# The token chain ahead of cross-attention in two groups beside self-attention, with transposes, V and K of the context in the last self-attention steps, and the second layer's last q one unit earlier

## The chip, the cores and the metric

The kernel runs on one core of one Trainium2 chip. The metric is the device time of one execution in microseconds, in the median of several runs. Engines are named as in the profile: PE is TensorE (PEld its weight loads), DVE is VectorE, ACT is ScalarE, POOL is GpSimd, SP is the engine that issues most of the DMAs.

## What is computed

There are 8 units (batch entries) with 56 latent rows of 128 channels each, and a context of 1500 rows per unit. Everything is float32, with 16 heads of 8 channels:

```python
x = x + mha(ln(x), ln(x))                    # self-attention, 56 rows with 56 rows of the same unit
x = x + mha(ln_q(x), ln_kv(ctx))             # cross-attention, 56 rows with 1500 rows
h = ln(x); gates = softmax(top2(h @ rw.T + rb))
x = x + sum_e gates[e] * (gelu(h @ fc1[e].T) @ fc2[e].T + b2[e])     # 8 experts
x = x + attn(ln(x), ctx; bit_quant(Wq, Wk, Wv, Wo))                  # second cross-attention
```

## The kernel before

The 448 latent rows lie in four token tiles of 112 rows, so that a tile holds two units: tile 0 has units 0 and 1. Each engine has a program written out by hand, and semaphores tie the programs together; an engine takes its instructions strictly in their order, and a wait holds up all that is queued behind it.

**Self-attention** runs in `SA_STEPS` = 12 steps. In step i the scores of batch i are made, batch i-1 is transposed, batch i-2 is multiplied with the values, batch i-3 is transposed back and normalised, and batch i-4 comes out as columns of `attnT`. The table `SA_PIECES` puts work on the context between these: "t" is `transpose_ctx` of a third of a unit, "k" is `project_k` of a third. A piece's first instruction on PE waits until the last user of the bank `MI` has been evacuated (`prev`). DVE and POOL do the statistics of the context (`ctx_stats`, `ctx_aggregate`, `ctx_rstd`, `ctx_normalise`) between steps. K is split into three bf16 parts by ACT, POOL (`k_rest`), DVE (`k_second_part`) and POOL (`k_third_part`, which counts `k3_done`). When all three thirds of a unit are split, SP copies them by `restack` in two halves of six DMAs into `kst`.

**The first chain** follows for all four token tiles at once: `project_out(0)`, `add_projection(0)`, `token_stats(1)`, `token_rstd(1)`, `token_normalise(1)`, `transpose_tokens(1)`, `token_gain(1)`, `project_q(0)`, `split_q(0)` into three bf16 parts, `load_qall(0)` (six DMAs on SP) and `place_q` into `qst` for unit 0. PE also makes K of unit 1 here (`project_k_apart`).

**The start of the pass** makes `START_TILES` = 18 of unit 0's 24 maximum tiles (`max_tile` on PE, `reduce_tile` on DVE, four banks). V of unit 0 and the transposes of unit 2 stand between them. After tile 11 `max_parts` gives the maxima of the first half, `transpose_max` turns them after tile 15, and a DMA (`shift`) puts them beside q. The scores wait for it.

**A window** is the cross-attention of one unit in 12 steps: scores, exponentials, values, with the maximum tiles of the next unit (`STEP_TILES`; in the first window `FIRST_TILES`, which also has what is left of unit 0's), K of the unit after next in steps 0 to 2, V of the next in steps 4 to 6, and in the first layer transposes of a later unit in steps 9 to 11. On SP a window issues `place` and `restack` of the next unit's second half, a context load, and `place` and `restack` of the first half of the unit after it. `max_tile` waits at tile 0 and at tile 12 for the `kst` half that it reads. Eight windows make the first layer's pass, the experts follow, and eight windows the second's. There the last half of q (`split_q(2)`, `load_qall(2)`) is made in windows 1 and 2; unit 4 is the first to need it.

## Time and profile before

| | us |
|---|---|
| median of 3 runs | 582.97 (581.22 to 584.65) |
| the profiled execution | 581.15 |
| its span in the trace | 579.4 |
| PE busy | 528.1 (91%) |
| PE weight loads | 391.9 (68%) |
| DVE busy | 391.7 (68%) |
| ACT busy | 334.0 (58%) |
| POOL busy | 220.5 (38%) |

The share of the chain that ended last is 70% PE and 15% DVE. Matrix work on PE overlaps, so that its busy share is not its share of peak. The granted clock of PE is given as a part of full speed (1.0 is 2.4 GHz, 0.5 is 1.2 GHz); it is 0.946 over the whole span, and below full in the first quarter and in the slice around 456 us. In timelines, several like instructions in a row are merged into one row with their count, and the brackets at a row's end give how long the engine had stood and what ended it.

### The profile page before, as it was taken

The page shows a single profiled execution, that of the slowest core. Times are in us where ns is not written, and L with a number is a line of the kernel's source. Part 1 is how long each engine was busy: PE and PEld are TensorE (multiplying, and loading weights), DVE is VectorE, ACT ScalarE, POOL GpSimd, SP SyncE. Part 2 cuts the span into 40 slices and gives each one's busy share as a digit, 9 for nine tenths or more (in the row PEclk, how much of TensorE's full clock was granted, in tenths as well). Part 3 has the DMA queues.
Part 4 walks back from the last instruction along what each step waited for, and adds up shares of the span by engine and source line. Part 5 has one row for each costly group of instructions (what it writes and reads, how often), then busy time and mean ns, then how long its engine had stood idle before and what let it go on. Part 6 is the DMA issues. An engine that isn't in the chain of part 4 may idle for free.

```text
span 579.4 us, 16262 instructions
## 1 busy us (share of the span) xinstructions
PE 528.1 (91%) x6648; PEld 391.9 (68%) x6648; DVE 391.7 (68%) x976; ACT 334.0 (58%) x527; POOL 220.5 (38%) x217
## 2 busy tenths in 40 slices
PE   4699748789999999999989999999999899999996
PEld 2588525466767676776767998867677576767674
DVE  6565477767878888787742434888878477786730
ACT  1156322547686777766676444376666467675573
POOL 3549944473957677532251200031403032240000
PEclk9679877889999999999999999999999799999997
DMA  5110361734444554647546601005372826534300
GB/s 157 48 54 3 107 148 44 174 92 101 122 119 104 137 139 90 155 95 190 146 107 185 175 2 28 5 0 141 86 187 57 218 57 166 135 88 101 76 4 9
DMA packets 37870, 58.69 MB, mean 101 GB/s; under 512 B 17957, under 2 KB 21405, under 8 KB 37797
## 3 DMA queue, kind: packets, MB, share of 16 engines
q1 hardware_dynamic: 37476, 57.60, 39.5%
q8 instruction: 53, 0.87, 0.6%
q14 instruction: 21, 0.16, 0.1%
q10 hardware_dynamic: 320, 0.06, 0.1%
HBM read 17.81 MB, written 0.23 MB: 31 GB/s over the span
## 4 chain that ended last, share of the span: by engine, by line
PE 70%; DVE 15%; POOL 4%; DMA 3%; issue 3%; ACT 2%; SPq 2%; ACTq 0%; DVEq 0%; POOLq 0%
PE SM L1371 13%; PE PO L1386 13%; PE ST L1343 9%; DVE mxp L883 8%; PE MI L1292 8%; PE MI L1282 7%; PE ST L1564 4%; PE ST L1554 4%; PE MI L1271 2%; POOL cxs L518 2%; PE SM L1477 2%; DVE ksplit L878 1%; ACT pts L671 1%; DMA xT<-in_ctxT 1%; PE MI L1318 1%
## 5 line engine op out<-in xcount | busy, mean ns | idle before, releaser
L883 DVE TENSOR_REDUCE mxp<-SM 112x1 f32<-112x500 f32 x374 | 244.5, 674 | 77.5 <-PE SM L1371 76.3
L671 ACT ACTIVATE pts<-ST 128x896 f32<-128x896 f32 x192 | 171.3, 912 | 29.4 <-PE ST L1343 29.0
L1371 PE MATMUL SM<-kst,qst 96*112 96x500 bf16 x374 | 146.9, 401 | 11.6 <-DVE mxp L883 6.7
L527 POOL TENSOR_TENSOR kr<-kf,ksplit 128x500 f32<-128x500 f32 x48 | 54.9, 1144 | 173.1 <-ACT ksplit L636 173.1
L1343 PEld LDWEIGHTS ST<-qst,kst 98*128 98x128 bf16 x1536 | 95.5, 100 | 36.3 <-issue 12.4
L1343 PE MATMUL ST<-qst,kst 98*128 98x112 bf16 x1536 | 108.3, 214 | 2.2 <-DMA qst<-mrow 2.2
L1386 PE MATMUL PO<-pts,vaug 125*32 125x112 f32 x3072 | 97.3, 266 | 2.0 <-ACT pts L671 1.6
L1386 PEld LDWEIGHTS PO<-pts,vaug 125*32 125x32 f32 x3072 | 71.4, 111 | 24.3 <-issue 14.7
L1371 PEld LDWEIGHTS SM<-kst,qst 96*112 96x112 bf16 x374 | 48.5, 131 | 45.4 <-DVE mxp L883 29.1
L518 POOL TENSOR_SCALAR cxs<-cxs,cmv,crstd 125x128 f32<-125x128 f32 x84 | 66.8, 810 | 0.0
L648 ACT ACTIVATE vaug<-MI 125x512 f32<-125x512 f32 x48 | 28.7, 597 | 60.8 <-PE MI L1292 60.8
L532 POOL TENSOR_TENSOR ksplit<-kr,ksplit 128x500 bf16<-128x500 f32 x48 | 54.4, 1135 | 16.7 <-DVE ksplit L878 16.7
L1292 PE MATMUL MI<-watt,xT 128*125 128x128 f32 x384 | 56.1, 291 | 0.3 <-ACT vaug L648 0.3
L1292 PEld LDWEIGHTS MI<-watt,xT 128*125 128x125 f32 x384 | 47.6, 193 | 8.9 <-issue 5.3
L1282 PE MATMUL MI<-xT,watt 128*128 128x500 f32 x92 | 49.6, 621 | 1.3 <-ACT ksplit L636 0.8
L635 ACT ACTIVATE kf<-MI,vec 128x500 f32<-128x500 f32 x46 | 31.1, 677 | 33.6 <-PE MI L1282 33.6
L769 ACT ACTIVATE moe<-ST,vec 128x224 f32<-128x224 f32 x64 | 28.4, 447 | 34.8 <-PE ST L1554 33.8
L878 DVE CAST ksplit<-kr 128x500 bf16<-128x500 f32 x48 | 34.8, 726 | 10.2 <-POOL kr L527 10.2
L636 ACT ACTIVATE ksplit<-MI,vec 128x500 bf16<-128x500 f32 x46 | 30.8, 670 | 0.0
L623 ACT ACTIVATE xT<-MI,vec 128x500 f32<-128x500 f32 x24 | 18.4, 767 | 16.3 <-PE MI L1271 15.8
L506 POOL TENSOR_TENSOR xrstd<-xvar,half_neg 112x2 f32<-112x2 f32 (+1 forms) x6 | 4.9, 809 | 59.9 <-DVE xvar L809 59.9
L511 POOL TENSOR_TENSOR crstd<-cvar,half_neg 125x12 f32<-125x12 f32 x8 | 18.3, 2287 | 22.5 <-DVE cvar L865 22.5
(156 smaller groups left out, 546.2 us busy)
## 6 DMA issues: line engine op xcount, KB each, us to landing
kst<-ksplit SPq DMA_DIRECT2D x192, 187.5 KB, 3.6
cxs<-in_ctx SPq DMA_DIRECT2D x8, 750.0 KB
xT<-in_ctxT SPq DMA_DIRECT2D x8, 750.0 KB, 6.5
qst<-qall SPq DMA_DIRECT2D x56, 21.0 KB, 1.9
watt<-in_watt SPq DMA_DIRECT2D x1, 768.0 KB, 6.0
cxs<-in_w1T SPq DMA_DIRECT2D x3, 256.0 KB, 5.7
cxs<-in_w2T SPq DMA_DIRECT2D x3, 256.0 KB, 6.7
pts<-in_w1T SPq DMA_DIRECT2D x3, 256.0 KB, 5.9
```

The source lines that it names most:

```text
L518: last = nc.gpsimd.tensor_scalar(cx[n.par][:, c], cx[n.par][:, c], cmv[n.par][:, c, 0:1], crstd[n.par][:, c:c + 1], ALU.subtract, ALU.mult)
L527: nc.gpsimd.tensor_tensor(kr[:, c], kf[:, c], ksplit[n.par][:, 0, c], ALU.subtract).then_inc(kr_done, 1)
L532: nc.gpsimd.tensor_tensor(ksplit[n.par][:, 2, c], kr[:, c], ksplit[n.par][:, 1, c], ALU.subtract).then_inc(k3_done, 1)
L635: nc.scalar.activation(kf[:, c], bank[:, 0:THIRD], ACT.Identity, bias=bias_k(n.s + 1)).then_inc(k_evac, 1)
L671: nc.scalar.activation(PT[:, k % PTB], ST[:, k % 2, :, 0:4 * PC], ACT.Exp, scale=SCALE).then_inc(exp_done, 1)
L878: nc.vector.tensor_copy(ksplit[n.par][:, 1, c], kr[:, c]).then_inc(k2_done, 1)
L883: nc.vector.tensor_reduce(mxp[:, j // 3, j % 3:j % 3 + 1], tile_bank(j, banks), AX.X, ALU.max).then_inc(sm_red, 1)
L1282: mm(bank[:, 0:THIRD], watt[:, n.s + 1, 1], xT[n.par][:, THIRD * i:THIRD * (i + 1)], start=True, stop=True).then_inc(kp_full, 1)
L1292: last = mm(MI[0:KC, D * c:D * (c + 1)], xT[n.par][:, at:at + KC], watt[:, n.s + 1, 2], start=True, stop=True)
L1343: last = mm(ST[:, k % 2, cc, PC * p:PC * (p + 1)], kst[n.par][:, 4 * half + p, at:at + 128], qst[n.par][:, 4 * half + p], start=True, stop ...
L1371: mm(tile_bank(j, banks), qst[n.par][0:SROWS, j // 3], kst[n.par][0:SROWS, j // 3, at:at + THIRD], start=True, stop=True).then_inc(sm_full, 1)
L1386: last = mm(PO[32 * p:32 * p + 32, PC * half:PC * (half + 1)], vaug[n.par][:, c, at:at + 32], PT[0:KC, k % PTB, cc, PC * p:PC * (p + 1)], ...
```

## The change

The first chain is cut into two groups (`PARTS`): token tile 0, and token tiles 1 to 3. The first group's steps stand in self-attention's steps 6 to 8: `project_out(0)` and the transposes of unit 1's first third in step 6, `transpose_tokens(1)` and `project_q(0)` in step 7, `split_q(0)` in step 8. `SA_PIECES` further takes the transposes of unit 1 in steps 6, 8 and 9, V of unit 0 in steps 8 to 10 and K of unit 1 in steps 10 and 11, one third each. On DVE `ctx_stats(u2)` moves from step 6 to 7 and its `ctx_aggregate` from step 7 to 8; POOL's `ctx_rstd(u2)` stays in its step 8, ahead of the last `k_third_part` of unit 0. The second group's steps stand between the maximum tiles of unit 0, of which there are now 21 ahead of the pass. SP issues `load_qall(0)` behind both halves of `restack(u0)`, then the context load of unit 3, and `load_qall(1)` behind `restack(u1, 0)`. The statistics of unit 3 move to tile 12 and to steps 3 and 4 of the first window. In the second layer the last q goes from steps (1,9) to (2,5) to steps (1,3) to (2,0), and `load_qall(3)` moves from the middle of SP's window 2 to the end of its window 1. The other lines renumber groups and semaphore counts, and are left out below.

```diff
 Q2_STEP, Q1_STEP = 1, 10
-START_TILES = 18
+START_TILES = 21
 def spread_tiles(own, per):
...
 OWN_MX_STEP, NEXT_MX_STEP = 1, 6
-FIRST_TILES = spread_tiles(TILES - START_TILES, (3, 3, 3, 3, 2, 2, 3, 3, 2, 2, 2, 2))
+FIRST_TILES = spread_tiles(TILES - START_TILES, (3, 3, 3, 3, 2, 2, 2, 2, 2, 2, 2, 1))
 FIRST_OWN_MX_STEP, FIRST_NEXT_MX_STEP = 3, 8
 OUT_AT, LN_AT, ROUTER_AT, GATES_AT, B2_AT = (5, 10), (6, 10), (6, 11), (7, 9), (7, 11)
-LN5_AT, Q2_AT = (1, 9), (1, 10)
-SPLIT2_AT = ((1, 11), (2, 4), (2, 5))
+LN5_AT, Q2_AT = (1, 3), (1, 9)
+START_OUT, START_ADD, START_NORM, START_LN, START_Q, START_SPLIT = 3, 3, 10, 12, 15, (16, 17, 18)
+SPLIT2_AT = ((1, 10), (1, 11), (2, 0))
 TERNARY_AT = ((4, 5), (4, 6), (4, 7), (4, 9), (4, 10), (4, 11), (5, 4), (5, 5), (5, 6), (5, 7), (5, 9))
...
 SA_PIECES = {1: (("t", 0, 0), ("t", 0, 1)), 2: (("t", 0, 2),), 3: (("k", 0, 0),), 4: (("k", 0, 1),),
-             5: (("k", 0, 2),), 7: (("t", 1, 0),), 8: (("t", 1, 1),), 9: (("t", 1, 2),)}
+             5: (("k", 0, 2),), 6: (("out", 0, 0), ("t", 1, 0)), 7: (("ln", 0, 0), ("q", 0, 0)),
+             8: (("t", 1, 1), ("v", 0, 0)), 9: (("t", 1, 2), ("v", 0, 1)), 10: (("v", 0, 2), ("k", 1, 0)),
+             11: (("k", 1, 1), ("k", 1, 2))}
 class Unit:
...
         window(Unit(s, None, u))
+PARTS = (range(0, 1), range(1, TT), range(0, HT), range(HT, TT), range(0, HT), range(HT, TT))
...
 def token_tiles(n):
-    return range(TT) if n < 2 else range(HT * (n % 2), HT * (n % 2 + 1))
+    return PARTS[n - 1] if n else range(TT)
...
+def token_slice(ts):
...
+    return slice(ts[0], ts[-1] + 1)
...
+def token_cols(ts):
...
+    return slice(TP * ts[0], TP * (ts[-1] + 1))
 def build_kernel(nc, x_in, ctx_in, ctxT_in, watt_in, vec_in, rows_in, rwT_in, w1T_in, w2T_in, b2_in,
...
             def load_qall(n):
-                cols = slice(0, N) if n == 0 else slice(HN * (n - 1), HN * n)
+                cols = token_cols(Q_TILES[n])
                 for part, ready in enumerate((q1_ready, q2_ready, q3_ready)):
...
             def place(n, half):
-                if n.s == 0 and n.c == 1:
-                    sp.wait_ge(qall_loaded, 16 * TERMS)
+                if n.s == 0 and n.c in (1, 2):
+                    sp.wait_ge(qall_loaded, 16 * TERMS * n.c)
                 if n.s == 1 and n.c in (1, B // 2):
-                    sp.wait_ge(qall_loaded, 16 * TERMS * (2 + n.c // (B // 2)))
+                    sp.wait_ge(qall_loaded, 16 * TERMS * (3 + n.c // (B // 2)))
                 if n.s or n.c >= 2:
...
                     restack(nxt, 1)
-                if n.s == 1 and n.c == 2:
-                    load_qall(2)
                 if n.s == 0 and (n + 4).exists():
...
                     load_xT(xT_unit)
+                if n.s == 1 and n.c == 1:
+                    load_qall(3)
                 if n.s == 0 and n.c in (3, 4):
...
             load_ctx(Unit(0, None, 2))
-            load_ctx(Unit(0, None, 3))
             restack(u0, 0)
...
             load_qall(0)
+            load_ctx(Unit(0, None, 3))
             place(u1, 0)
             restack(u1, 0)
+            load_qall(1)
             run_windows(0, window)
...
                     k_parts(k_unit, None)
+                if n.first():
+                    ctx_rstd(n + 3)
                 if n.s == 0 and (n + 3).exists():
...
                 if n.s == 0 and n.c == 5:
-                    token_rstd(2)
+                    token_rstd(3)
                 if n.s == 1 and n.c == 0:
-                    token_rstd(5)
+                    token_rstd(6)
             pool.wait_ge(padded, 1)
...
                     ctx_rstd(u1)
+                if i == 6:
+                    token_rstd(1)
                 if i == 8:
...
                     ctx_normalise(u1, (i - 4,))
-                if i in (9, 10):
-                    ctx_normalise(u0 + 2, (i - 9,))
+                if i == 9:
+                    ctx_normalise(u0 + 2, (0,))
                 for kind, unit, third in SA_PIECES.get(i - 1, ()):
-                    if kind == "k":
+                    if kind == "k" and unit == 0:
                         k_rest(u0, third)
                 for kind, unit, third in SA_PIECES.get(i - 3, ()):
-                    if kind == "k":
+                    if kind == "k" and unit == 0:
                         k_third_part(u0, third)
-            token_rstd(1)
+            k_parts(u1, None, lambda: ctx_normalise(u0 + 2, (1,)))
+            token_rstd(2)
             ctx_normalise(u0 + 2, (2,))
-            k_parts(u1, None)
-            ctx_rstd(u0 + 3)
             run_windows(0, window)
-            token_rstd(3)
+            token_rstd(4)
             gates_exp(1)
-            token_rstd(4)
+            token_rstd(5)
             run_windows(1, window)
...
                     evac_xT(n, (third,))
-                else:
+                if kind == "k":
                     evac_k(n, third)
+                if kind == "v":
+                    evac_v(n, third)
             for i in range(SA_STEPS):
...
                     evac_piece(*pieces[1])
-            for i in range(3):
-                evac_k(u1, i, K_BANKS[i])
             start_pass()
...
                 if half == 0:
-                    dve.wait_ge(qall_loaded, 16 * TERMS * (n.s + 1))
+                    dve.wait_ge(qall_loaded, 16 * TERMS * (2 * n.s + 1))
                     dve.wait_ge(ld_member, 32)
...
                 dve.wait_ge(op_full, n + 1)
-                t = slice(0, TT) if n == 0 else slice(HT * ((n - 1) % 2), HT * ((n - 1) % 2 + 1))
+                t = token_slice(PARTS[n])
                 width = D * (t.stop - t.start)
-                bank = MI if n in (1, 3) else PO
+                bank = PO if n % 2 else MI
                 nc.vector.tensor_tensor(xt[:, t], xt[:, t], bank[0:TP, 0:width].rearrange("p (t d) -> p t d", d=D),
...
                     if n.s == 1 and (n.c, k) == (0, 9):
-                        token_stats(5)
+                        token_stats(6)
                     if n.s == 1 and (n.c, k) == (0, 11):
-                        token_normalise(5)
+                        token_normalise(6)
                     if n.s == 1 and (n.c, k) == LN5_AT:
-                        token_gain(5)
+                        token_gain(6)
                     if n.s == 1 and (n.c, k) in SPLIT2_AT:
-                        split_q(2, (SPLIT2_AT.index((n.c, k)),))
+                        split_q(3, (SPLIT2_AT.index((n.c, k)),))
                     if n.s == 1 and (n.c, k) == OUT_AT:
-                        add_projection(3)
+                        add_projection(4)
+                    if n.first() and k == 3:
+                        ctx_stats(n + 3, range(6, NCH))
+                    if n.first() and k == 4:
+                        dve.wait_ge(cstat_ready, (n + 3).count(1, 1))
+                        ctx_aggregate(n + 3)
                     if ln_unit is not None:
...
                                             ).then_inc(sa_sub, 1)
+                if i == 6:
+                    add_projection(0)
+                    token_stats(1)
+                if i == 7:
+                    token_gain(1)
+                if i == 8:
+                    split_q(0)
                 if 0 <= i - 3 < B:
                     normalise(SM[:, 1], sa_pot, sa_rden, sa_norm, i - 2, i - 2, (i - 3) % 2)
+                if i == 6:
+                    token_normalise(1)
                 for kind, unit, third in SA_PIECES.get(i - 2, ()):
-                    if kind == "k":
+                    if kind == "k" and unit == 0:
                         k_second_part(u0, third)
...
                     ctx_aggregate(u1)
-                if i == 6:
+                if i == 7:
                     ctx_stats(u0 + 2, every)
-                if i == 7:
+                if i == 8:
                     dve.wait_ge(cstat_ready, (u0 + 2).count(1, 1))
                     ctx_aggregate(u0 + 2)
-            add_projection(0)
-            token_stats(1)
-            token_normalise(1)
-            ctx_stats(u0 + 3, range(5))
-            token_gain(1)
-            split_q(0)
-            ctx_stats(u0 + 3, range(5, NCH))
-            dve.wait_ge(cstat_ready, (u0 + 3).count(1, 1))
-            ctx_aggregate(u0 + 3)
...
             first = u0
             place_q(first, 0)
+            place_q(first, 1)
             for j in range(START_TILES):
                 reduce_tile(first, j, banks=4)
-                if j == 3:
-                    place_q(first, 1)
-                if j in (1, 4, 7):
-                    k_second_part(first + 1, j // 3)
+                if j == START_ADD:
+                    add_projection(1)
+                    token_stats(2)
+                if j == START_NORM:
+                    token_normalise(2)
+                if j == START_LN:
+                    token_gain(2)
+                if j in START_SPLIT:
+                    split_q(1, (START_SPLIT.index(j),))
+                if j in (0, 4, 7):
+                    k_second_part(first + 1, (0, 4, 7).index(j))
                 if j == TILES // 2 - 1:
                     max_parts(first, 0)
+                if j == TILES // 2:
+                    ctx_stats(u0 + 3, range(6))
             run_windows(0, window)
...
                 return v_evac, n.count(3, i + 1)
...
-            def project_k_apart(n, prev):
...
-                for i in range(3):
-                    last = project_k(n, i, prev, K_BANKS[i])
-                return last
             def transpose_max(n, half):
...
                     return transpose_ctx(n, third, prev)
-                return project_k(n, third, prev)
+                if kind == "k":
+                    return project_k(n, third, prev)
+                if kind == "out":
+                    pe.wait_ge(ld_rows, 48)
+                    return project_out(0, (sa_att, 2), prev)
+                if kind == "ln":
+                    return transpose_tokens(1, prev)
+                if kind == "q":
+                    return project_q(0, prev)
+                return project_v(n, third, prev)
             for i in range(SA_STEPS):
...
                     transpose_po(SM[:, 1]).then_inc(sa_pot, 1)
-            pe.wait_ge(ld_rows, 48)
-            project_out(0, (sa_att, B))
-            prev = project_k_apart(u1, prev)
-            transpose_tokens(1)
             pe.wait_ge(padded, 1)
             pe.wait_ge(ld_ones, 32)
-            project_q(0, 1)
...
             for j in range(START_TILES):
                 max_tile(u0, j, banks=4)
-                if j in (1, 4, 7):
-                    prev = project_v(u0, j // 3, prev)
-                if j in (10, 13, 16):
-                    prev = transpose_ctx(u0 + 2, (10, 13, 16).index(j), prev)
+                if j == START_OUT:
+                    project_out(1, (sa_att, B))
+                if j == START_LN - 1:
+                    prev = transpose_tokens(2, prev)
+                if j == START_Q - 1:
+                    prev = project_q(1, prev)
+                if j in (5, 8, 17):
+                    prev = transpose_ctx(u0 + 2, (5, 8, 17).index(j), prev)
                 if j == TILES // 2 + 3:
```

## Rows read from the trace of the kernel before

**Rows 1.** Windows: stretch, length, busy (count) per engine PE to POOL; clock, DMA, GB/s.

```profile
67.60:88.40 20.80, 11.76 (x29) 6.11 (x29) 10.97 (x47) 3.63 (x6) 11.36 (x14) 0.66 0.66 160
88.40:103.40 15.00, 12.10 (x55) 8.41 (x55) 12.67 (x26) 4.34 (x7) 6.74 (x5) 0.81 0.29 64
```

**Rows 2.** The chain that ended last, 67 to 104 us: start, length, step.

```profile
85.48 2.36 DMA qall<-qsplit
...
88.38 1.08 PE ST L1371 x2
...
99.67 0.22 PE ST L1308
...
100.19 3.18 DMA qst<-mrow
```

**Rows 3.** Timeline of POOL, 50 to 68 us: start, length, operation, idle before.

```profile
54.98 3.37 POOL L518 TENSOR_SCALAR cxs<-cxs,cmv,crstd 125x128 f32<-125x128 f32 x4
...
63.02 2.29 POOL L511 TENSOR_TENSOR crstd<-cvar,half_neg 125x12 f32<-125x12 f32 x1 [1.38 <-DVE cvar L865]
65.28 1.14 POOL L532 TENSOR_TENSOR ksplit<-kr,ksplit 128x500 bf16<-128x500 f32 x1
```

**Rows 4.** Timeline of SP's queue, 66 to 86 us.

```profile
66.44 9.86 SPq L412 DMA_DIRECT2D kst<-ksplit  x12
82.31 3.76 SPq L393 DMA_DIRECT2D qall<-qsplit  x6
```

**Rows 5.** Timeline of VectorE, 55 to 62 us.

```profile
55.36 2.41 DVE L855 BATCH_NORM_STATS2 cstat<-cxs 125x6 f32<-125x128 f32 x12
...
59.49 2.43 DVE L878 CAST ksplit<-kr 128x500 bf16<-128x500 f32 x1
```

**Rows 6.** Windows by stage: the six microseconds around and behind the first tile.

```profile
88.00:94.00 6.00, 5.62 (x22) 4.81 (x23) 4.29 (x11) 0.60 (x1) 2.22 (x2) 0.50 0.05 7
```

**Rows 7.** Timeline of TensorE in the first 90 us: pieces at half clock.

```profile
28.66 1.70 PE L1491 MATMUL ST<-ident,p_sa 112*56 112x112 f32 x8
...
67.74 0.74 PE L1234 MATMUL PO<-watt,attnT 128*112 128x128 f32 x2 [0.49 <-ACT attnT L740]
...
89.25 1.91 PE L1292 MATMUL MI<-watt,xT 128*125 128x128 f32 x8
```

**Rows 8.** Timelines of VectorE and POOL: reductions, and a subtraction beside POOL's.

```profile
97.66 1.25 DVE L883 TENSOR_REDUCE mxp<-SM 112x1 f32<-112x500 f32 x2
...
110.23 1.14 DVE L895 TENSOR_TENSOR mparts<-nmx,mparts 112x4 bf16<-112x4 f32 x1
...
110.22 1.13 POOL L527 TENSOR_TENSOR kr<-kf,ksplit 128x500 f32<-128x500 f32 x1 [1.59 <-ACT ksplit L636]
```

**Rows 9.** Timeline of TensorE, 415 to 457 us (second half).

```profile
415.67 1.14 PE L1292 MATMUL MI<-watt,xT 128*125 128x128 f32 x8
...
441.42 0.38 PE L1371 MATMUL SM<-kst,qst 96*112 96x500 bf16 x1
...
456.12 0.64 PE L1371 MATMUL SM<-kst,qst 96*112 96x500 bf16 x1 [2.13 <-issue]
```

**Rows 10.** Windows by stage: second half, windows of units 1 and 2.

```profile
407.21:431.99 24.78, 24.52 (x360) 17.49 (x359) 19.27 (x38) 16.59 (x26) 6.73 (x6) 1.00 0.52 127
431.99:461.50 29.51, 26.86 (x357) 18.13 (x356) 19.73 (x39) 17.01 (x26) 6.72 (x6) 0.90 0.60 145
```

**Rows 11.** Timeline of VectorE, 415 to 435 us.

```profile
415.12 1.34 DVE L878 CAST ksplit<-kr 128x500 bf16<-128x500 f32 x1 [0.17 <-POOL kr L527]
...
429.87 0.44 DVE L838 TENSOR_SCALAR qf<-MI,vec 128x224 f32<-128x224 f32 x1
...
431.67 2.67 DVE L883 TENSOR_REDUCE mxp<-SM 112x1 f32<-112x500 f32 x4
```

**Rows 12.** SP's queue at 434 us, and landing of `kst` copies, 420 to 460.

```profile
434.60 11.12 SPq L393 DMA_DIRECT2D qall<-qsplit  x6
...
DMA to landing us min/median/max: 2.8/3.8/5.0
```

96 lines of the change are left out of this document (46 added, 50 removed).

## The prediction

> **What bounds the kernel now.** I read from coarse to fine: the busy shares of the page, the busy time by stage, the chain of waits through the first 104 us, then the timelines of the engines on it. In the long middle TensorE is full, and a link shortened elsewhere is worth nothing there. The stages that the change touches are different: between 67.6 and 88.4 us TensorE is busy 11.76 of 20.80 us, and between 88.4 and 103.4 it is 12.10 of 15.00, at a granted clock of 0.81 [rows 1]. The reader is to see in the chain that this time is a row of small links: self-attention ends, the token chain follows, q is split, six `qall` copies are issued, the last lands 2.36 us after its issue at 85.48, and the first maximum tile is made at 88.38. At 99.67 the maxima of the first half are transposed, their shift takes 3.18 us by DMA from 100.19, and unit 0's scores follow at once, at 103.4 [rows 2]. So two things count at the start: when the first tile is made, and how long it is from there to the scores (15.0 us).
>
> **What gates the first tile after the change.** q of the first token tile is now early, but its `qall` copies stand on SP behind both halves of `restack(u0)`, which wait for `k3_done`, the last third part of unit 0's K. Before, that part ends at 65.28 + 1.14 = 66.42 [rows 3] and SP starts its twelve copies at 66.44 [rows 4]. On POOL it stands behind `ctx_rstd(u2)` (2.29 us [rows 3]), which waits for VectorE's aggregate of unit 2; this order stays. The change moves that aggregate from step 7 to step 8 of self-attention and puts new links ahead of it:
> - Up to step 6 nothing is late. `token_rstd(1)` of one column goes ahead of POOL's 3.37 us of normalising; I take 0.6 us, about a quarter of the 2.29 that twelve columns take (between nothing and 2.29) [rows 3]. VectorE's small token steps lie in its gaps. The last `k_second_part` of unit 0 took 2.43 us while POOL made two subtractions, ending at 61.92 [rows 5]; now 62.5.
> - `ctx_stats(u2)`, 2.41 us, before at 55.36 in step 6 [rows 5], now comes after it: 64.9. `split_q(0)` follows; its first operation (0.3 to 0.4; 224 columns take 0.44 [rows 11]) ends at 65.3.
> - TensorE's step 8 begins with a transpose piece that waits for that `qf_ready`; queued behind it are the transposes of batch 7, the output of batch 4, the values of batch 6, V's first third and the back-transpose of batch 5. By the order of its queue TensorE has stood since about 59.6. After such a wait the clock is low: 0.50 from 88 to 94 us, behind the wait for the first tile [rows 6]. At that level the transposes of a batch take 1.70 and a V third 1.91 [rows 7]; the first piece has half as many passes as V, 1.0, and the three small ones some 2: together 6.5. At full clock V takes 1.14 [rows 9] and the whole some 4.3. I take 6.5, as the pause is nearly as long: 71.8.
> - VectorE normalises batch 5 (0.6) and aggregates unit 2 (1.1, as between the end of the cast and POOL's start at 63.02 [rows 3, 5]): 73.5. POOL: 2.29 + 1.14: `k3_done` at 77.0, **10.6 us later** than now.
> - SP: twelve copies 9.86, six `qall` copies 3.2 to the last issue [rows 4] and 2.36 to landing, 0.54 from there to the first tile [rows 2]: 93.0 instead of 88.38, **+4.6 us**. The context load that now shares the queue with the restack moves behind it; if that is what makes a copy 0.82 instead of 0.7, it saves up to 1.
>
> The pieces' K and V are hidden below this chain: by the queues they end near 84. With a punctual `k3_done` they would be next in line.
>
> **From the first tile to the scores.** Three V thirds of 1.91 us leave this stretch [rows 7], but VectorE sets it. Up to the first maxima it has twelve reductions of 0.6 to 0.67 [rows 8] and three casts, as before. New: after tile 3 `project_out(1)` of three token tiles, twelve passes of 0.37 at half clock ([rows 7]: 0.74 for two, the next in line at the same pace), 4.2 us, at full clock half; VectorE stands 2.4 us for it, since `add_projection(1)` is in its queue with tile 4 behind. Then addition and statistics 1.8, normalising 1.2 (its rstd waits on POOL for unit 1's third parts, done near tile 10). Taken off: 1.25 of present waits for V and `place_q`. Sum +4.15. Behind the maxima, `transpose_max` now stands on TensorE behind `project_q(1)`, which waits for a reduction and `token_gain(2)`: 0.6 + 0.6 + 0.9 = 2.1. VectorE also has to reduce up to tile 16, with six chunks of statistics and a part of the split, before TensorE can pass tile 20: 0.9 more. **+7.2 us**, between +3 (full clock, the waits overlapping) and +9: scores near 115.2.
>
> A rule bears on this stretch. A four-column `mparts` subtraction was held 1.14 us when a POOL subtraction had begun 0.01 us earlier, and both ended together [rows 8]. The Trainium skill (SBUF — State Buffer, section SBUF: two separate sides) says that VectorE and GpSimd share a port pair as an exclusive lock held for a whole instruction, also against VectorE operations with two SBUF inputs. POOL now normalises unit 2 just when the first maxima are split; by this rule that adds one of POOL's instructions, 0.8 us, without it nothing. It is left out of the sum.
>
> **Unit 0's window** loses three tiles (1.8 us of VectorE) and gains half of unit 3's statistics and its aggregate (1.2 + 1.1), partly in waits; its first tile waits for VectorE's backlog. Between -3 and +1 I take **-1.0**. POOL's later work for unit 3 ends before step 9 needs it. `load_qall(1)` stands on SP ahead of `place(u1,1)` and `restack(u1,1)`; these land some 5 us before tile 12 of unit 1 is due.
>
> **The last q.** In the second half the window of unit 2 shows the cost of the present order: 29.51 us against 24.78 [rows 10]. SP stands inside `load_qall(2)`, 11.12 us [rows 12], so unit 4's `restack` is late: TensorE stands 2.13 us before its first tile [rows 9], then runs at half clock. That is 4.7 us to be had. But the copies now stand ahead of `place` and `restack` of unit 3's second half. Their last part is ready only after the first three tiles of that window: two of the four reductions from 431.67, and a subtraction of 0.4: 433.5 [rows 11]. Three copies of 0.63 and six of 0.82 [rows 4] end at 440.3; the last lands 3.8 after its issue [rows 12]: 443.3. Tile 12 is due at about 441.4 [rows 9]: 2 us idle instead of 2.13, and I price the slow clock behind it alike: **-0.3 net**, between -4.7 (no new stall) and +1. Also `token_gain(6)` of step 3 stands behind a cast that ends at 416.46 [rows 11]; the V third of 415.67 [rows 9] now waits for it until 417.0: **+1.3**, with nothing (if TensorE's lead grows) and +3 (a lower clock) as bounds.
>
> **Sum.** 4.6 + 7.2 - 1.0 - 0.3 + 1.3 = 11.8 us. The profiled execution took 581.15 (span 579.4): 593.0. The median of the runs shown, 582.97, is 1.8 above it; I forecast 595 for the median.
>
> **Rivals.**
> - Lower ends: the last q gains in full and step 8 runs at full clock: 11.8 - 4.4 - 2.2 = 5.2, or 588. For it: the margin of tile 12 is 2 us; against it: the clock after every long wait in these stages. Chance 0.22.
> - The order of work is as told, but the token steps fall into waits that VectorE has anyway (it is idle 2.3 us from 88.4 to 103.4 [rows 1], which speaks against it): +2 for the stretch, 590 less what the last q gives, 585 to 590. Chance 0.12.
> - Faster. `k3_done` is not late, because VectorE has aggregated unit 2 before TensorE's step 8 closes the circle. Then the first tile comes at about 84 (-4.5, bounded by the pieces), the stretch is no longer than now, as V has left it, and the last q gives -4.7 but +1.3: 575. It decides at a `k3_done` of about 69; at 77.0 it is 8 us past that. Against it stands the order of the queues, which is in the code. That q in two groups doesn't come earlier at all is part of the forecast. Chance 0.10.
> - The forecast's own case, 590 to 602: 0.56.
>
> The range, 583 to 602, takes in the first two rivals and leaves out the third and some of the upper tail. About 0.5% can be told from no change in this kernel: slower by more 0.78, within 0.12, faster 0.10.
>
> **What would show it.** In the profile after: SP's twelve `kst` copies begin near 77, not 66.4; TensorE stands over 4 us until about 65 and goes on with a transpose piece, released by VectorE's `qf`; the first tile near 93, the scores near 115; in the second half a gap before tile 12 of unit 3, none before unit 4's first. If the copies begin before 70 or the scores before 106, the main step is wrong.

## The result and the profile after

The changed kernel took 592.25 us in the median of 4 runs (587.04 to 593.01), the kernel before 583.29 on the same chip: a ratio of 1.0159, 95% interval 1.0104 to 1.0214. The profiled execution took 592.01 us (span 590.2), 10.9 more than that of before. The forecast of 595 and its sign held. Its main term, the first chain, held almost to the tenth; two smaller terms did not, and one loss was not in it, so that the closeness of the total is in part luck (the section on why the prediction was right has the account).

The timelines of the changed kernel's start, with start, length, operation and the wait ahead of it. TensorE:

```profile
63.73 1.09 PE L1301 MATMUL MI<-ident,cxs 125*128 125x125 f32 x4 [5.12 <-DVE qf L857]
64.62 1.70 PE L1524 MATMUL ST<-ident,p_sa 112*56 112x112 f32 x8
...
67.43 2.07 PE L1322 MATMUL MI<-watt,xT 128*125 128x128 f32 x8
...
87.05 2.04 PE L1312 MATMUL MI<-xT,watt 128*128 128x500 f32 x2 [1.05 <-ACT ksplit L657]
92.10 1.05 PE L1395 MATMUL ST<-kst,qst 96*112 96x500 bf16 x2 [3.02 <-DVE qst L926]
...
114.60 0.95 PE L1367 MATMUL ST<-qst,kst 98*128 98x112 bf16 x8
```

GpSimd and SP's queue over the same stretch:

```profile
72.09 2.29 POOL L529 TENSOR_TENSOR crstd<-cvar,half_neg 125x12 f32<-125x12 f32 x1 [11.26 <-DVE cvar L884]
74.35 1.13 POOL L550 TENSOR_TENSOR ksplit<-kr,ksplit 128x500 bf16<-128x500 f32 x1
```

```profile
75.51 9.99 SPq L430 DMA_DIRECT2D kst<-ksplit  x12
85.55 4.59 SPq L411 DMA_DIRECT2D qall<-qsplit  x6
```

This is the circle that the prediction went round: TensorE stands 5.12 us for q of the first group, then works through its step at half clock; VectorE gets batch 5 late, aggregates unit 2 late, and GpSimd's rstd, which waits 11.26 us for that, comes ahead of the third part of K, because that is the order of its queue. The twelve `kst` copies begin at 75.51 instead of 66.44 [rows 4], the first tile comes at 92.10 instead of 88.38 [rows 2], the scores at 114.60 instead of 103.4. Windows of TensorE (stretch, length, busy, clock, DMA share, GB/s) show no full clock from 78 us to the scores:

```profile
78.00:92.10 14.10, 9.19 (x24) 0.50 0.74 161
92.10:103.00 10.90, 10.90 (x32) 0.50 0.20 71
103.00:114.60 11.60, 7.38 (x20) 0.50 0.47 107
```

Two executions must be laid side by side with care, since self-attention comes to one and the same step up to 6.5 us earlier or later from one to the next, although the code up to there differs in no more than the place of one context load on SP. The table below measures from a fixed point, the scores of batch 6 of self-attention on TensorE (their start is the column "SA"): to the first tile, to unit 0's scores; then from the scores to unit 0's output (ScalarE's copy of it out of the bank `PO`), and in the second layer from unit 0's output to unit 4's, which holds all that the last q touches. "Before" is one trace. The medians come from four chips: the kernel before had 583.3 beside `after`; 581.8 beside `lastq_alone`, `pool_first`, `stats_late` and `both`; 582.6 beside `after_again`, `first_chain_alone`, `split_only` and `both_v_out`; 583.5 beside the other four.

| kernel | SA | to first tile | to scores | to unit 0's output | second layer, 0 to 4 | median |
|---|---|---|---|---|---|---|
| before | 50.42 | 37.96 | 53.00 | 34.73 | 103.60 | 583.3 |
| lastq_alone | 51.74 | 38.99 | 53.81 | 31.94 | 100.59 | 577.6 |
| split_only | 47.35 | 38.68 | 54.28 | 31.93 | 98.40 | 573.5 |
| split_again | 50.41 | 39.10 | 53.68 | 32.07 | 98.66 | 574.4 |
| after | 48.99 | 43.11 | 65.61 | 31.92 | 106.21 | 592.3 |
| after_again | 47.47 | 43.26 | 65.76 | 31.94 | 101.29 | 591.4 |
| first_chain_alone | 47.67 | 43.04 | 65.55 | 31.95 | 104.73 | 593.2 |
| pool_first | 50.49 | 39.91 | 62.23 | 31.96 | 101.81 | 584.7 |
| stats_late | 51.64 | 42.42 | 64.93 | 31.95 | 100.67 | 588.1 |
| both | 53.90 | 37.57 | 60.06 | 31.97 | 100.90 | 583.2 |
| v_out_alone | 51.78 | 41.72 | 66.63 | 32.10 | 102.13 | 589.3 |
| both_v_out | 47.51 | 30.24 | 54.35 | 32.06 | 100.76 | 576.4 |
| combo | 48.81 | 30.50 | 54.72 | 32.08 | 98.74 | 574.2 |
| combo_t | 48.98 | 30.49 | 57.00 | 33.73 | 98.90 | 577.9 |

The first four kernels have the same code up to the second layer. Their scores come 53.0 to 54.3 after the fixed point, those of the change 65.6 in three traces: the first chain costs **11.9 us** there (65.6 less the mean of 53.7). From unit 0's output to the second layer's first output all 14 take 267.1 to 267.8 us.

### The profile page after: what moved, and what is told of

It reads as the page before. It is cut to its first block, busy times and chain, and to the rows that moved or that the text cites. A ratio compares the mean times of both kernels' runs of the same rounds, so it can differ in the third digit from the quotient of the medians.

```text
span 590.2 us, 16288 instructions
## 1 busy us (share of the span) xinstructions
PE 535.0 (91%) x6650; PEld 394.0 (67%) x6650; DVE 391.4 (66%) x984; ACT 333.6 (57%) x527; POOL 220.8 (37%) x218
## 4 chain that ended last, share of the span: by engine, by line
PE 67%; DVE 16%; SPq 5%; POOL 4%; DMA 4%; issue 3%; ACT 2%; ACTq 0%; DVEq 0%; POOLq 0%
PE SM L1395 12%; PE PO L1410 11%; DVE mxp L902 8%; PE ST L1367 8%; PE MI L1322 7%; PE MI L1312 7%; PE ST L1595 4%; PE ST L1585 4%; SPq L430 3%; DMA xT<-in_ctxT 2%; PE SM L1510 2%; PE MI L1301 2%; POOL cxs L536 2%; DVE ksplit L897 1%; DVE cstat L874 1%
## 5 line engine op out<-in xcount | busy, mean ns | idle before, releaser
L545 POOL TENSOR_TENSOR kr<-kf,ksplit 128x500 f32<-128x500 f32 x48 | 54.7, 1139 | 188.7 <-ACT ksplit L657 188.7
L1367 PEld LDWEIGHTS ST<-qst,kst 98*128 98x128 bf16 x1536 | 95.5, 100 | 34.7 <-issue 13.5
L1410 PE MATMUL PO<-pts,vaug 125*32 125x112 f32 x3072 | 95.3, 262 | 2.1 <-ACT pts L692 1.6
L1410 PEld LDWEIGHTS PO<-pts,vaug 125*32 125x32 f32 x3072 | 69.9, 109 | 24.0 <-issue 14.5
L1312 PE MATMUL MI<-xT,watt 128*128 128x500 f32 x96 | 55.6, 663 | 5.3 <-DMA xT<-in_ctxT 2.6
L656 ACT ACTIVATE kf<-MI,vec 128x500 f32<-128x500 f32 x48 | 32.5, 677 | 44.8 <-PE MI L1312 44.8
L657 ACT ACTIVATE ksplit<-MI,vec 128x500 bf16<-128x500 f32 x48 | 32.1, 669 | 0.0
L1301 PE MATMUL MI<-ident,cxs 125*128 125x125 f32 x96 | 18.1, 321 | 10.1 <-DVE qf L857 6.0
```

The source lines that it names most:

```text
L545: nc.gpsimd.tensor_tensor(kr[:, c], kf[:, c], ksplit[n.par][:, 0, c], ALU.subtract).then_inc(kr_done, 1)
L656: nc.scalar.activation(kf[:, c], bank[:, 0:THIRD], ACT.Identity, bias=bias_k(n.s + 1)).then_inc(k_evac, 1)
L1312: mm(bank[:, 0:THIRD], watt[:, n.s + 1, 1], xT[n.par][:, THIRD * i:THIRD * (i + 1)], start=True, stop=True).then_inc(kp_full, 1)
L1367: last = mm(ST[:, k % 2, cc, PC * p:PC * (p + 1)], kst[n.par][:, 4 * half + p, at:at + 128], qst[n.par][:, 4 * half + p], start=True, stop ...
L1410: last = mm(PO[32 * p:32 * p + 32, PC * half:PC * (half + 1)], vaug[n.par][:, c, at:at + 32], PT[0:KC, k % PTB, cc, PC * p:PC * (p + 1)], ...
```

## The experiments

My theory was that the step of GpSimd's rstd of unit 2, kept ahead of the last third part of K, carries the delay of the first tile; that TensorE's wait for q and its half clock are what makes that rstd late; and that the last q gives back little. The rivals were that VectorE's statistics alone make it late, that the pieces of V and K themselves hold the first tile, and that the last q gives more or less than forecast.

### Two orders turned, one at a time and together

`pool_first`, on the changed kernel, lets GpSimd finish K of unit 0 before the rstd of unit 2:

```diff
-                if i == 8:
-                    ctx_rstd(u0 + 2)
...
                         k_third_part(u0, third)
+                if i == 8:
+                    ctx_rstd(u0 + 2)
```

> The changed kernel with one edit on POOL: in self-attention's step 8 the last third part of unit 0's K stands ahead of the rstd of unit 2. Theory (the late k3_done holds the first tile): SP's twelve kst copies begin at about 62.4 us instead of 75.5, because the third part needs only the cast that ends at 61.1; the first tile then no longer waits for q but for TensorE's own queue, whose last K piece ends at 89.1, so it comes at about 89.2 instead of 92.1, and the time falls by 3 us against the changed kernel. Rival (the copies are not what holds the tile, or POOL's order is free): kst copies or first tile unmoved, time the same.

Measured: 584.7 us, ratio 1.0034 (1.0004 to 1.0063). SP's queue, and then TensorE, of this kernel:

```profile
63.85 10.15 SPq L430 DMA_DIRECT2D kst<-ksplit  x12
74.05 5.12 SPq L411 DMA_DIRECT2D qall<-qsplit  x6
```

```profile
65.23 1.10 PE L1301 MATMUL MI<-ident,cxs 125*128 125x125 f32 x4 [5.14 <-DVE qf L857]
...
88.57 2.04 PE L1312 MATMUL MI<-xT,watt 128*128 128x500 f32 x2 [1.05 <-ACT ksplit L657]
90.40 1.04 PE L1395 MATMUL ST<-kst,qst 96*112 96x500 bf16 x2
```

One order turned in GpSimd's program moves the `kst` copies from 26.5 to 13.4 us behind the fixed point, as the expectation had it. The first tile gains only 3.2 of these 13.2 us (43.11 to 39.91), because TensorE comes to it straight from its last piece, with no wait in the brackets. This shows both the main step and the next limit.

`stats_late` puts VectorE's `ctx_stats(u2)` behind the split of q, in step 8:

```diff
-                if i == 7:
+                if i == 8:
                     ctx_stats(u0 + 2, every)
-                if i == 8:
```

> The changed kernel with one edit on VectorE: the statistics of unit 2 stand in step 8 behind the split of q instead of in step 7 ahead of it. Theory: TensorE's wait of 5.1 us ahead of the transpose piece shrinks to about 2.7 and its clock need not fall for long; the back-transpose of batch 5 comes at about 65 instead of 69.4, the aggregate ends at 69.5 instead of 72.0, kst copies begin at about 73, first tile at about 89.5: 2.5 us less than the changed kernel. Rival (the statistics only trade places and the aggregate ends when it did): kst copies at 75.5 and no gain.

Measured: 588.1 us, 1.0096 (1.0065 to 1.0127).

```profile
64.06 0.65 PE L1300 MATMUL MI<-ident,cxs 125*128 125x125 f32 x4 [2.82 <-DVE qf L857]
```

TensorE's wait for q falls from 5.12 to 2.82 us, and the clock falls all the same, to 0.50 from 65.5 us on. And the statistics stand in front of the aggregate either way: the `kst` copies begin 25.7 us behind the fixed point instead of 26.5, and the first tile gains only 0.7 where 2.5 were expected. The theory of the statistics alone falls.

`both` has the two edits together.

> The changed kernel with both edits, POOL's order and VectorE's. Theory: each alone is capped by the other chain, together they free both: kst copies at about 62.5, TensorE's pieces end by about 77 to 80, the last qall copy lands at 79, first tile near 80 instead of 92.1, and the time is about 12 us less than the changed kernel, near 580 and so at or below the kernel before. Rival (what follows the first tile absorbs it, since VectorE has its backlog anyway): the first tile is earlier but the scores move by less than half of that.

Measured: 583.2 us, 1.0029 (0.9987 to 1.0071). I had expected the first tile near 80 us and about 580 us, and missed both. The rival, that the scores would move by less than half of what the tile gains, missed too: the tile gains 5.5 us and the scores 5.6. Its TensorE:

```profile
66.33 1.09 PE L1300 MATMUL MI<-ident,cxs 125*128 125x125 f32 x4 [2.82 <-DVE qf L857]
...
89.65 2.03 PE L1311 MATMUL MI<-xT,watt 128*128 128x500 f32 x2 [1.05 <-ACT ksplit L657]
91.47 1.04 PE L1394 MATMUL ST<-kst,qst 96*112 96x500 bf16 x2
```

The queries were placed at 86.4. From 66.33 to 91.47 TensorE goes through two transposes of the context, three V and three K pieces at half clock, 2.03 to 2.07 us for each third of V or K and some of them behind a 1.0 us wait for the evacuation of the one bank `MI`. The pieces, which my prediction had ending near 84 and hidden, ended at 89.1 in the changed kernel, 3 us before the first tile: hidden there, and the limit as soon as `k3_done` is punctual. What the prediction left out is that TensorE stands 3.9 us in all in five waits between them, for ScalarE to evacuate `MI` (0.99, 0.99, 0.40, 0.44 and 1.05 in the changed kernel).

### The two parts of the change apart

`lastq_alone` is the kernel before with the new places of the last q.

```diff
-LN5_AT, Q2_AT = (1, 9), (1, 10)
-SPLIT2_AT = ((1, 11), (2, 4), (2, 5))
+LN5_AT, Q2_AT = (1, 3), (1, 9)
+SPLIT2_AT = ((1, 10), (1, 11), (2, 0))
...
-                if n.s == 1 and n.c == 2:
-                    load_qall(2)
...
+                if n.s == 1 and n.c == 1:
+                    load_qall(2)
```

> The kernel before with only the last q's part of the change: token_gain in step (1,3), q in (1,9), its split in (1,10), (1,11), (2,0), the qall copies at the end of SP's window 1. Theory from the profile after: the 2.1 us wait with 2.7 us of slow clock in front of unit 4's first tile goes; in its place come 1 us at V's first third and 1.7 us ahead of tile 12 of unit 3, neither with a fall of the clock: 2.5 to 3 us less than the kernel before. A wait of 2.2 us for xT at unit 4's window with 2.9 us of slow clock may come with it, if it belongs to the change: then +2.5 us. If that wait is chance, it is here only in some runs.

Measured: 577.6 us, 0.9926 (0.9892 to 0.9960): 4.1 us faster in the medians, 3.0 in the traced stretch. Expected were 2.5 to 3. Both waits that I had foreseen are there, in its TensorE timeline:

```profile
416.15 1.14 PE L1292 MATMUL MI<-watt,xT 128*125 128x128 f32 x8 [0.94 <-DVE hT L827]
...
443.34 0.39 PE L1371 MATMUL SM<-kst,qst 96*112 96x500 bf16 x1 [1.54 <-issue]
```

What the prediction had not foreseen, and the expectation took from the profile after, is that the clock stays full behind the second wait: TensorE is at 1.00 from 441 to 448 us. The slow clock was the expensive half of the old wait: 2.13 us [rows 9] in a window 4.7 us too long [rows 10].

`first_chain_alone` is the changed kernel with the last q where it was before.

> The changed kernel with its last q put back to where it was before (unit 9 and 10), so that the first chain is all that differs from the kernel before. Theory A, the two parts add up, the last q gives 4 us and the first chain costs the 8.4 us by which unit 0's last output is late in the profiled run: about 591 us, ratio 1.014. Theory B, the forecast's sum, in which the last q gave nothing: as the changed kernel, 592 us or 588 us where its late load is chance, less what the last q gives, so no more than that.

Measured: 593.2 us, 1.0167 (1.0107 to 1.0228), 1.8 above the change itself on the same chip, as theory A has it: the first chain is the whole loss. Its second layer has the old wait again, now 1.98 us ahead of a first tile, and 5 us behind it a late load of `xT`, the transposed context that K and V are made from; the window from 463.79 us on is at a clock of 0.51:

```profile
462.43 0.39 PE L1395 MATMUL SM<-kst,qst 96*112 96x500 bf16 x1 [1.98 <-issue]
...
467.47 2.00 PE L1312 MATMUL MI<-xT,watt 128*128 128x500 f32 x2 [3.33 <-DMA xT<-in_ctxT]
```

```profile
463.79:470.00 6.21, 2.88 (x8) 0.51 0.89 203
```

### The late xT

The profiled run of the change lost 5.3 us in unit 4's window of the second layer, where the change has no hand: a load of xT landed after 8.2 us, 2.20 us late. `after_again` is the changed kernel unaltered.

> The changed kernel itself once more. In its profiled run the window of unit 4 of the second half (492.0 to 520.3 us) took 29.7 us against 24.4 in the kernel before, behind a load of xT that landed 2.2 us late and a half clock after it. Theory A, that wait is chance: here the window takes 24.4 to 25.3 us, and the median is about 587 us (ratio 1.008). Theory B, it belongs to the changed kernel: 29 us again and about 592 us (ratio 1.016).

Measured: 591.4 us, 1.0125 (1.0059 to 1.0190). The same place in the profiled runs of both, `after` first:

```profile
493.12 2.01 PE L1312 MATMUL MI<-xT,watt 128*128 128x500 f32 x2 [2.20 <-DMA xT<-in_ctxT]
```

```profile
489.43 1.08 PE L1312 MATMUL MI<-xT,watt 128*128 128x500 f32 x2 [0.89 <-DMA xT<-in_ctxT]
```

The second trace is the one of theory A (window 25.56 us), the median is the one of theory B. Read together: this load is due about when it lands, in the changed kernel and in others (0.6 in `pool_first`, 0.9 in `split_again`, 0.8 in `combo`), and it costs about 1 us or 5, by whether the clock falls behind it. `split_again` does not have the change at all, so the lateness is not the change's own. The 8 runs of the changed kernel lie in two groups, 586.0 and 587.0, and six from 591.2 to 593.0; the traced ones, 585.96 and 592.01, lie 6.1 apart, of which 4.9 are the second layer's stretch. That the other runs part at the same place is likely, but no trace shows it. The medians of the variants point the same way. The changed kernel is 9.0 and 8.8 us above before on its chip, `pool_first` 2.9, `stats_late` 6.3 and `both` 1.4. These are gains of about 6.0, 2.6 and 7.5 us, where the scores come only 3.4, 0.7 and 5.6 us sooner; none of these three traces has a wait for xT of over 1 us. What the medians gain beyond the scores stays open.

### What else the first chain needs

`both_v_out` takes the three V pieces out of self-attention, on top of `both`, and puts them behind first tiles 1, 2 and 4 (the evacuations on ScalarE, left out below, move with them).

```diff
-             8: (("t", 1, 1), ("v", 0, 0)), 9: (("t", 1, 2), ("v", 0, 1)), 10: (("v", 0, 2), ("k", 1, 0)),
+             8: (("t", 1, 1),), 9: (("t", 1, 2),), 10: (("k", 1, 0),),
...
+                if j in (1, 2, 4):
+                    prev = project_v(u0, (1, 2, 4).index(j), prev)
```

> The changed kernel with both orders turned (GpSimd's third parts of K ahead of the rstd of unit 2, VectorE's statistics behind the split of q) and with the three V pieces of unit 0 taken out of self-attention and put behind first tiles 1, 2 and 4. Theory A, TensorE's eight pieces at half clock, one after another through the one bank MI, are the last limit of the first tile: it comes at 86.5 us (on self-attention's own start in the run of both orders), as soon as the queries are placed, the scores 5 us earlier, and the median is about 578 us. Theory B, what is taken out costs as much among the first tiles: scores as before at 114 us, median 583 us.

Measured: 576.4 us, 0.9884 (0.9809 to 0.9959), as theory A. The first tile comes 7.3 us sooner than in `both` (30.24 after the fixed point for 37.57) and the scores 5.7 sooner. Its TensorE, and the window behind the first tiles:

```profile
74.37 2.03 PE L1313 MATMUL MI<-xT,watt 128*128 128x500 f32 x2 [1.05 <-ACT ksplit L657]
77.75 1.05 PE L1396 MATMUL ST<-kst,qst 96*112 96x500 bf16 x2 [1.35 <-DVE qst L928]
...
85.34 1.04 PE L1323 MATMUL MI<-watt,xT 128*125 128x128 f32 x8
```

```profile
83.00:91.00 8.00, 6.37 (x36) 1.00 0.04 12
```

With V among the tiles TensorE has the full clock from 83 to 91 us, and the third V piece takes 1.04 us instead of 2.07. Then it stands 3.07 us for VectorE's `xn`, and from 96 us to the scores the clock is 0.50 again. In the changed kernel the 10.90 us behind the first tile were busy throughout and stayed at 0.50.

`v_out_alone` takes out V and turns neither order.

> The changed kernel with only the three V pieces of unit 0 taken out of self-attention and put behind first tiles 1, 2 and 4; both orders (GpSimd's, VectorE's) as in the change. Theory A, the first tile is held by the placed queries, which come through the third parts of K behind GpSimd's rstd, and TensorE's pieces only reach as far as that by accident: the first tile does not move against self-attention's own start (43 us after its last scores but one), TensorE waits over 8 us ahead of it in place of 3, and the median stays at 589 to 593 us. Theory B, the pieces at half clock are the whole cost of the first chain: scores 11 us earlier as with both orders turned, 577 to 580 us.

Measured: 589.3 us, 1.0131 (1.0066 to 1.0195). TensorE now stands where its pieces were:

```profile
80.96 2.04 PE L1314 MATMUL MI<-xT,watt 128*128 128x500 f32 x2 [1.05 <-ACT ksplit L657]
93.50 1.05 PE L1397 MATMUL ST<-kst,qst 96*112 96x500 bf16 x2 [10.51 <-DVE qst L928]
```

So the late `k3_done` is the first limit and the pieces the second, and to lift the second alone gives the first tile 1.4 us and the scores nothing (66.6 after the fixed point for 65.6).

What stays as it was in all these runs is the stretch from the first tile to the scores: 22.3 to 22.5 us, and 24.1 to 24.9 with V among the tiles, where the kernels with before's start have 14.6 to 15.6. Its later part begins with VectorE's addition of the second group, here in the changed kernel:

```profile
97.93 0.55 DVE L949 TENSOR_TENSOR xt<-xt,PO 112x384 f32<-112x384 f32 x1 [2.39 <-PE PO L1265]
```

From that addition to the scores `after`, `after_again` and every variant so far that has the new first chain take 16.5 to 16.7 us. TensorE's clock does not set this: `after` has half clock throughout, and `v_out_alone` takes the same 16.67 us with this in it:

```profile
104.00:110.00 6.00, 2.63 (x15) 0.97 0.12 36
```

VectorE is busy for 11.02 of the last 11.60 us before the scores of `after`, which fits the prediction's reading that its queue paces the stretch. No run takes work from it there, so that this half of the loss is argued and not shown.

### The best of both halves

`split_only` is the kernel before with one line changed, the last q's splits; its projection and its copies stay where they were.

```diff
-SPLIT2_AT = ((1, 11), (2, 4), (2, 5))
+SPLIT2_AT = ((1, 11), (2, 0), (2, 1))
```

> The kernel before with the last q's three splits at (1,11), (2,0), (2,1) in place of (1,11), (2,4), (2,5), and nothing else moved: projections and loads stay where they were. Theory A, what the last q gave was the 2.1 us wait ahead of unit 4's first tile and the slow clock behind it (window 29.5 in place of 25 us): 577 us, as with the whole second part of the change alone (577.6), and both new waits of that (0.9 us for V, 1.5 us ahead of tile 12) are absent: down to 576 us. Theory B, the loads still come too late here, since the SP queue has 6 loads of 0.8 us ahead of the placing: 581 to 583 us.

Measured: 573.5 us, 0.9843 (0.9779 to 0.9906). That is beyond theory A. SP's queue and the windows of unit 2 and then of unit 1 in this kernel:

```profile
424.71 5.10 SPq L412 DMA_DIRECT2D kst<-ksplit  x6
429.86 3.82 SPq L393 DMA_DIRECT2D qall<-qsplit  x6
437.06 1.26 SPq L428 DMA_DIRECT2D qst<-qall  x2
```

```profile
425.60:449.74 24.14, 23.88 (x355) 1.00 0.60 147
400.83:425.60 24.77, 24.51 (x359) 1.00 0.52 131
```

SP is through `load_qall` in 3.82 us instead of 11.12 [rows 12], since q is ready when it gets there, and the copies stand behind `restack` of the next unit, where they hold up nobody. `split_again` repeats it.

> The kernel before with only the last q's splits moved, once more, beside the kernels above on one chip. Theory A, its gain is the second half's 5.2 us (98.4 in place of 103.6 us) and the rest of its 9 us was an earlier start of self-attention by chance: 576 to 578 us, ratio 0.990. Theory B, the 9 us are its own: 573 to 574 us, ratio 0.984.

Measured: 574.4 us, 0.9852 (0.9780 to 0.9924). The medians are theory B's, 9 us; the traces show 4.9 and 5.2 us in the second layer, and 2.7 and 2.8 in unit 0's first window, which has the same code as before. The kernel before was traced once, and with its clock at 0.72 from 114 to 120 us; if its other runs have that too, these parts add up to 8, but no further trace of it was taken, and what is beyond the second layer's 5 us stays open.

`combo` is `both_v_out` with these splits.

> Both orders turned and the V pieces out (576.4 us), and the last q with only its splits moved, to (1,11), (2,0), (2,1), in place of the change's. Theory A, the two halves of the program add: the second half takes 98.4 us from its first output to unit 4's, as with the splits alone, in place of 100.8 us, median 574 us. Theory B, the splits alone owed their 573.5 us to an early self-attention and a full clock: no difference, 576 to 577 us.

Measured: 574.2 us, 0.9884 (0.9802 to 0.9966), on a chip where `split_again` had 574.4. Its second layer is that of `split_only` (98.74), as theory A says. But the repaired first chain is worth nothing beside the one-line kernel: its first tile is 8.2 us earlier than in before's start, and its scores 1.0 us later (54.7 for a mean of 53.7), since the stretch between them is 9.2 us longer (24.2 for 15.0). `combo_t` tries one link of the stage in between, the third transpose of unit 2's context behind tile 10 instead of 17.

> The same, with the third transpose of unit 2's context behind first tile 10 in place of 17, so that it no longer waits ahead of unit 0's scores for the second group's q. Theory A, that transpose and its wait (0.8 + 1.1 us in the run before) stand ahead of the scores: these come 2 us earlier, median 572 us. Theory B, the scores are held by the landed maxima or by VectorE's reductions of the tiles ahead of them: no difference, 574 us.

Measured: 577.9 us, 0.9947 (0.9902 to 0.9991), a miss of both theories: slower than `combo`, by 2.3 us at the scores and 1.7 more in unit 0's window. The transpose now waits for GpSimd, and the whole second group behind it:

```profile
97.19 1.06 PE L1301 MATMUL MI<-ident,cxs 125*128 125x125 f32 x4 [5.78 <-POOL cxs L536]
```

## Why the prediction was right, step by step

- **First tile, +4.6.** Measured +5.15 against before's trace, 4.4 against the mean of the four kernels with its start (38.7). Of the links, TensorE's step at half clock took 6.7 us (6.5 forecast), its wait ended at 63.73 on an early self-attention (65.3), the rstd began 1.4 us earlier than forecast for the same reason, and `k3_done` was 9.1 late instead of 10.6 by the clock of the two traces; from the fixed point the copies begin 10.5 us late (26.52 for 16.02). `pool_first` and `both` show the order behind it.
- **First tile to scores, +7.2.** Measured +7.46. `add_projection(1)` came after a wait of 2.39 us (2.4 forecast), and the whole stage stayed at half clock. Up to the split of the first maxima it took 3.9 us more (4.15 forecast) and from there 3.6 more (3.0 forecast); the transpose of the maxima came 3.26 us behind them, as it now stands behind `project_q(1)`. The forecast's bound of +3 for full clock is contradicted by `both_v_out` and `v_out_alone`: where the clock was full for a part of the stretch, the addition's wait was 1.54 and 1.59 us instead of 2.39, and nothing behind the addition was shorter.
- **Unit 0's window, -1.0.** Measured -2.81 against before's trace, and nothing against the three other kernels with the same start: 31.93 to 32.07, and 31.92 here. The step that failed is taking the 34.7 us of one trace as the kernel's own. It was a slow clock behind 114 us, which none of the three shows. Before's:

```profile
114.00:120.00 6.00, 5.55 (x62) 0.72 0.15 61
```

- **The V third, +1.3.** The wait was 0.94 us for `hT`, but the window grew by only 0.42.
- **The last q, -0.3.** This term was mis-sized. The wait ahead of tile 12 of unit 3 was forecast at 2 us and came at 1.71, in this timeline of the changed kernel:

```profile
452.43 0.39 PE L1395 MATMUL SM<-kst,qst 96*112 96x500 bf16 x1 [1.71 <-issue]
```

  I priced the slow clock behind it like that of the old wait. The clock did not fall, and the windows of units 2 and 3 are 1.77 and 1.30 us shorter: with the V third's window -2.65, where the two terms made +1.0. `lastq_alone` gives -3.0 in the same stretch. But the price was right for a wait that is a little longer. `v_out_alone` has the same last q, and there it was 2.09 us:

```profile
456.63 0.39 PE L1397 MATMUL SM<-kst,qst 96*112 96x500 bf16 x1 [2.09 <-issue]
```

  The clock was at 0.50 from 458 us on, and unit 2's window took 27.78 us, as long as before's 27.67. In the eight traces with this last q the wait is 1.16 to 2.09 us, and only the longest had the slow clock. The lower rival ("the last q gains in full and step 8 runs at full clock") was nearly right in its first half (it asks for -3.4 together with the V third's wait, and -2.3 to -3.0 came) and wrong in its second.
- **Not forecast:** the late xT, +5.3 in the profiled run and near nothing in the second; self-attention's early start, -1.4; the tail, -0.5.

Against the table the sum reads 11.9 for the first chain, 0 for unit 0's window, -2.3 for the second layer without the late xT (101.29 for 103.60): 9.6 us, where the medians differ by 9.0 and 8.8. The two errors in my sum, +1.0 that was -2.3 and -1.0 that was nothing, leave the forecast 2 us too high.

This agreement is in part luck. The two traced executions of the changed kernel are 10.8 and 4.7 us longer than before's in their spans, with first chains equal to 0.15 us. The first of them came near the 593.0 of the forecast because a late xT that I did not have (+5.3) stood against the window of unit 0 (-2.8), the windows that the last q touches (-2.7) and self-attention's early start (-1.4). And the 9.6 us leave the late xT out: if six of the eight runs have it, as their times suggest, the terms add up to about 14 us where the medians differ by 9. The kernel before was traced in one execution, so the rest can't be placed.

The signs of the forecast came: the copies at 75.5 us (77), TensorE's wait ended by `qf`, the first tile at 92.1 (93), the scores at 114.6 (115), a gap ahead of tile 12 of unit 3 and none before unit 4's first tile. The faster rival asked for a `k3_done` of about 69 and a first tile at 84; `pool_first` had the copies begin at 63.9 and got the tile at 90.4, since that rival's bound of 84 from the pieces was itself 5 us too early.

## What to carry to other kernels

When work is moved forward into an emptier stretch, look at what the moved steps wait for: one wait in an in-order queue delays all that is queued behind it, here the step of TensorE that VectorE's aggregate and then GpSimd's rstd waited for, and the rstd stood ahead of the critical third part of K only because it had always stood there. Turn such an order before counting the gain, and expect the filler that hid beside it to be the next limit. And before a part of a change is taken over whole, try its smallest piece: of all that was moved here, one line with three split times gave the whole gain. Measure terms from a fixed point of the kernel, and against more than one trace of it.

## What the runs showed of the hardware

**The clock behind a wait.** In full stretches TensorE's granted clock stayed at 1.00 (2.4 GHz) behind waits of 0.89, 1.54 and 1.71 us, and fell to 0.50 (1.2 GHz) at the end of one of 2.20 us (0.50 from 493.1 to 499 us of the changed kernel), 1.4 us behind the one of 1.98 in `first_chain_alone`, and within 1.4 us of the end of the one of 2.09 in `v_out_alone`; before's own 2.13 us belongs to the second kind [rows 9, 10]. The difference in price is large: the 1.71 us wait stands in a window of 25.90 us, 1.8 longer than that of `split_only` (24.14), the 2.20 us one in a window 5.3 us longer. That these waits themselves decided is not shown; TensorE's work ahead of them differs too. And in the first stage of the changed kernel TensorE was busy in all of 10.90 us and still at 0.50, where in `both_v_out` a stretch busy 6.37 of 8.00 us had 1.00. Being busy by the profile was not what decided.

**Which instructions of GpSimd hold VectorE's small subtraction.** Two timelines of the changed kernel, VectorE and then GpSimd:

```profile
106.95 0.16 DVE L914 TENSOR_TENSOR mparts<-nmx,mparts 112x4 bf16<-112x4 f32 x1
...
120.35 0.98 DVE L914 TENSOR_TENSOR mparts<-nmx,mparts 112x4 bf16<-112x4 f32 x1
```

```profile
104.77 3.25 POOL L536 TENSOR_SCALAR cxs<-cxs,cmv,crstd 125x128 f32<-125x128 f32 x4
...
120.14 1.17 POOL L545 TENSOR_TENSOR kr<-kf,ksplit 128x500 f32<-128x500 f32 x1 [12.12 <-ACT ksplit L657]
```

The four-column subtraction took 0.16 us in the middle of GpSimd's normalising, and 0.98 when a GpSimd subtraction of 500 columns was under way; both ended within 0.02 us. It ran in 0.16 us too in five places beside the 2.29 us rstd, a GpSimd `TENSOR_TENSOR` of 12 columns that had begun about 1.5 us before. The Trainium skill (SBUF — State Buffer, section SBUF: two separate sides) has the lock held for a whole instruction by whichever of the two sides starts first. The long subtraction agrees with that, the normalising and the 12-column rstd don't, and the 0.8 us that I had left out of the sum by the rule were rightly left out.
